# A second Newton step in the reciprocal square root, and QKV weight transfers issued ahead of the LayerNorm loops, in an adaLN transformer layer on eight cores

## What is computed

```python
mod = (_silu(L0_c) @ L0_wmod).reshape(4, 6, 1, -1)      # sa, ca, ga, sb, cb, gb
h = _layernorm(x) * (1 + ca) + sa
q, k, v = h @ Wq.T + bq, h @ Wk.T + bk, h @ Wv.T + bv    # 16 q heads, 8 kv heads of 128
q, k = rope(q), rope(k)
def _softmax_kernel(x, R):
    n = jnp.sqrt(jnp.sum(x * x, axis=-1, keepdims=True))
    x = x / jnp.maximum(n, 1e-06)
    p = jnp.einsum('...d,ed->...e', x, R)
    feats = jnp.concatenate([jnp.sin(p), jnp.cos(p)], axis=-1)
    return feats / math.sqrt(F)
kv = einsum('bhsf,bhsd->bsfd', kp, v);  out = einsum('bhsf,bsfd->bhsd', qp, kv)
x = x + ga * (out @ Wo.T + bo)
h = _layernorm(x) * (1 + cb) + sb
x = x + gb * (sum of top-2 experts of h + shared expert of h)
```

## Time and profile before

| | us |
|---|---|
| median of the 2 timed runs | 3984.06 |
| lowest, highest | 3969.1, 3999.03 |
| profiled execution, its own time | 3891.31 |
| span of its slowest core (core 2) | 3889.8 |
| spans of all eight cores | 3820.8 to 3889.8 |
| TensorE busy, core 2 | 2504.4 (64%) |
| VectorE busy | 1339.4 (34%) |
| ScalarE busy | 379.8 (10%) |
| GpSimd busy | 170.3 (4%) |

### The profile page before, as it was taken

The page is one execution under the profiler, slowest core; times in us unless marked ns, Lnnn a source line. Parts: engine busy times, 40 slices in busy tenths (PEclk is TensorE's granted clock), DMA queues, the critical chain, the costliest instruction groups (busy, mean ns, idle before and its releaser), DMA issues.

```text
span 3889.8 us, 32080 instructions; the slowest of 8 cores (3820.8 to 3889.8 us)
## 1 busy us (share of the span) xinstructions
PE 2504.4 (64%) x10824; PEld 1081.6 (28%) x10824; DVE 1339.4 (34%) x2408; ACT 379.8 (10%) x422; POOL 170.3 (4%) x294
## 2 busy tenths in 40 slices
PE   4349821223972333683399579985899589976886
PEld 1124311111431111231144233432344234432332
DVE  0456255655613454436422022221222122211203
ACT  0121212121111111102100000000000000000000
POOL 0000000000000111000000000000000000000000
PEclk7559955555986566795599789998999899988997
DMA  9513100102334543610143864448543864457547
GB/s 164 103 54 65 25 26 15 28 25 46 65 55 82 103 74 75 165 23 0 41 90 65 169 225 109 87 71 256 159 92 65 200 217 87 92 110 230 159 83 262
DMA packets 84939, 395.09 MB, mean 102 GB/s; under 512 B 7184, under 2 KB 7440, under 8 KB 75312
## 3 DMA queue, kind: packets, MB, share of 16 engines
q0 software_dynamic: 41536, 208.26, 30.8%
q1 hardware_dynamic: 33696, 146.98, 10.8%
q10 hardware_dynamic: 9552, 37.80, 2.8%
HBM read 538.26 MB, written 46.20 MB: 150 GB/s over the span
## 4 chain that ended last, share of the span: by engine, by line
PE 50%; DMA 25%; DVE 13%; issue 8%; ACT 3%; DVEq 0%; POOL 0%; ACTq 0%; POOLq 0%; SPq 0%
PE pb L1034 23%; PE pb L612 9%; PE pb L1110 8%; DMA AW<-wmod 8%; DMA AW<-w2i 5%; DMA AW<-w2scr 4%; PE pb L902 3%; DMA w2scr<-AW 3%; DMA AW<-w1i 2%; DVE AMS L780 2%; PE pb L429 2%; DVE AMS L1122 2%; PE pb L578 1%; PE pb L548 1%; DVE AHT L583 1%
## 5 line engine op out<-in xcount | busy, mean ns | idle before, releaser
L1034 PE MATMUL pb<-AHT,AW 128*128 128x512 bf16 x4608 | 1007.4, 381 | 69.4 <-DMA AW<-w1i 48.5
L1110 PE MATMUL pb<-AW,AOT 128*128 128x512 bf16 x2304 | 586.6, 420 | 287.7 <-DMA AW<-w2i 150.2
L1034 PEld LDWEIGHTS pb<-AHT,AW 128*128 128x128 bf16 x4608 | 450.6, 98 | 626.0 <-issue 94.2
L1110 PEld LDWEIGHTS pb<-AW,AOT 128*128 128x128 bf16 x2304 | 239.9, 106 | 634.5 <-issue 422.2
L612 PE MATMUL pb<-AW,AHT 128*128 128x512 bf16 x1536 | 350.8, 382 | 0.0
L1122 DVE TENSOR_TENSOR AMS<-pb,AMS 128x2048 f32<-128x2048 f32 x40 | 91.7, 2292 | 718.8 <-PE pb L1110 715.0
L578 PE MATMUL pb<-identf,AX 128*128 128x128 f32 x256 | 98.3, 445 | 289.3 <-ACT AX L539 237.2
L429 PE MATMUL pb<-AW,scol 128*1 128x512 bf16 x384 | 135.0, 529 | 143.7 <-DMA AW<-wmod 128.5
L1058 ACT ACTIVATE AMS<-AMS 128x1024 f32<-128x1024 f32 x64 | 67.7, 1057 | 1469.5 <-DVE AMS L1055 1265.0
L1060 DVE TENSOR_TENSOR AMS<-pb,AMS 128x1024 f32<-128x1024 f32 x64 | 78.4, 1225 | 372.2 <-PE pb L1034 372.2
L612 PEld LDWEIGHTS pb<-AW,AHT 128*128 128x128 bf16 x1536 | 143.2, 98 | 182.1 <-issue 25.0
(11 more groups left out here) (148 smaller groups left out, 1649.8 us busy)
## 6 DMA issues: line engine op xcount, KB each, us to landing
AW<-w2scr SPq DMA_DIRECT2D x54, 2048.0 KB, 9.1
AW<-wmod POOLq DMA_DIRECT2D x24, 2048.0 KB, 19.2
w2scr<-AW ACTq DMA_DIRECT2D x18, 2048.0 KB
AW<-w1i POOLq DMA_DIRECT2D x32, 1024.0 KB, 9.3
AW<-w3i POOLq DMA_DIRECT2D x32, 1024.0 KB, 9.3
AW<-w2i POOLq DMA_DIRECT2D x16, 2048.0 KB, 22.5
AX<-xin SPq DMA_DIRECT2D x16, 1024.0 KB, 4.9
AW<-wqt POOLq DMA_DIRECT2D x4, 2048.0 KB, 19.1
```

The lines of the kernel that those rows point to most:

```text
L1034: ins = tt.matmul(pu[:, th * 512:(th + 1) * 512], slot(sl)[:, ic * 128:(ic + 1) * 128], ahtb[:, ic * 1024 + th * 512: ic * 1024 + (th + 1) ...
L1110: ins = tt.matmul(pw[:, ob * 512:(ob + 1) * 512], hebuf[:, hc * 1024 + tau * 128: hc * 1024 + tau * 128 + 128], slot(ws)[:, ob * 512:(ob + ...
```

## The change

Three edits. `emit_rsqrt` makes two Newton steps instead of one. The two GpSimd transfers of a QKV block (weights and bias row) move into a function `emit_qkv_wdma`, and those of blocks 0 and 1 of each half are emitted ahead of the loop that precedes that half's QKV: ahead of the LayerNorm loop for half 0, ahead of the middle of half 0 for half 1. The bias row goes round lanes 4 to 7 like the weights.

```diff
-            for _ in range(1):
+            for _ in range(2):
                 sch.op("vector", lambda v: v.tensor_mul(tmp_f, dst_f, dst_f),
...
-        def emit_qkv_block(sh, ob):
+        def emit_qkv_wdma(ob):
             wname, wbi = wsrc[ob]
             wkey = f"awblk{ob % 2}"
             sch.dma("gpsimd", lambda g, wname=wname, wbi=wbi, ob=ob: g.dma_start(
                 blkbuf(ob % 2)[:].rearrange("p (c n) -> p c n", c=NIC),
                 dram[wname][wbi]), lanes=(4, 5, 6, 7),
                 writes=W(ar_aw, wkey, (ob % 2) * 16384, (ob % 2 + 1) * 16384))
-            isq, isv = ob < 2, ob >= 4
             bsrc = ["bq", "bq", "bk", "bk", "bv", "bv"][ob]
             brow = brows[0:1, (ob % 2) * 512:(ob % 2) * 512 + 512]
-            brkey = f"brow{ob % 2}"
             sch.dma("gpsimd", lambda g, bsrc=bsrc, ob=ob, brow=brow: g.dma_start(
                 brow, dram[bsrc][0:1, (ob % 2) * 512:(ob % 2) * 512 + 512]),
-                writes=[brkey])
+                lanes=(4, 5, 6, 7), writes=[f"brow{ob % 2}"])
+
+        def emit_qkv_block(sh, ob, skip_dma=False):
+            if not skip_dma:
+                emit_qkv_wdma(ob)
...
+        emit_qkv_wdma(0)
+        emit_qkv_wdma(1)
         for t in range(8):
             emit_ln1_tile(0, t, True, None, lnxsA,
...
-            emit_qkv_block(0, ob)
+            emit_qkv_block(0, ob, skip_dma=(ob < 2))
...
+        emit_qkv_wdma(0)
+        emit_qkv_wdma(1)
         for t in range(8):
             if t:
                 emit_mid_B(0, t - 1)
...
-            emit_qkv_block(1, ob)
+            emit_qkv_block(1, ob, skip_dma=(ob < 2))
```

More of the change, by code:

```diff
@@ L595, in emit_qkv_block @@
                 writes=W(ar_aw, wkey, (ob % 2) * 16384, (ob % 2 + 1) * 16384))
-            isq, isv = ob < 2, ob >= 4
             bsrc = ["bq", "bq", "bk", "bk", "bv", "bv"][ob]
             brow = brows[0:1, (ob % 2) * 512:(ob % 2) * 512 + 512]
-            brkey = f"brow{ob % 2}"
             sch.dma("gpsimd", lambda g, bsrc=bsrc, ob=ob, brow=brow: g.dma_start(
                 brow, dram[bsrc][0:1, (ob % 2) * 512:(ob % 2) * 512 + 512]),
-                writes=[brkey])
+                lanes=(4, 5, 6, 7), writes=[f"brow{ob % 2}"])
+        def emit_qkv_block(sh, ob, skip_dma=False):
+            if not skip_dma:
+                emit_qkv_wdma(ob)
+            wkey = f"awblk{ob % 2}"
+            isq, isv = ob < 2, ob >= 4
+            brow = brows[0:1, (ob % 2) * 512:(ob % 2) * 512 + 512]
+            brkey = f"brow{ob % 2}"
             for t in range(8):
```

## The result

The changed kernel takes 3939.48 us (median of 13 runs), the kernel before 3902.73 (12 runs beside it, on the same chip): a ratio of 1.0099 with a 95% interval of 1.0072 to 1.0126. In some executions the cores of one die show a lower granted clock and the time is 70 to 190 us longer; ratios leave these out, and the two timed runs that I took as the level, 3999.03 and 3969.1, are as long as those. So the change costs 37 to 39 us where I forecast 14.4. Two errors of opposite sign stand behind that: the level is 81 us lower than the two runs had it, and the change costs 22 to 24 us more.

The account below looks back on a forecast made before the run. No engine is near full in the middle of half 0: one chain through VectorE, ScalarE and TensorE bounds it. Terms +17.4 + 1.0 - 4.0 + 0 + 0 = +14.4 us on 3984.06 gave 3998.5, range 3940 to 4045.

Parts of the forecast that it names:

- the level: Whole kernel: the median of two timed runs, 3984.06 us, taken as the time before, to which +14.4 was added.
- The second Newton step: Middle of half 0: four added operations cost 1.12 us on 128x16, 1.05 on 128x1; eight tiles give +17.4 us.
- the cover: Middle of half 1: added steps run beside modulation transfers whose waits swallow them; +1 us, bounds 0 and 9.0.
- The transfers of half 0: Before QKV of half 0: second weight block issued near 110, landing near 142.3, shortening VectorE's `xin` wait; 4 us off, bounds 0 and 5.9.
- The transfers of half 1: Middle of half 0: early weights gain nothing, and `v16` behind them still lands in time; cost 0, 8 us or more spare.
- `gac`: Output projection: the `wot` block now waits for the `gac` transfer on its lane; cost 0, with 40 us of cover.
- the 25 us: Middle of half 0: a sign of being wrong was growth under 10 or over 25 us; about 17 was expected.
- the 3 us: Middle of half 1: a sign of being right was its length staying as before within 3 us.
- runs stand otherwise than those two: Whole kernel: timed runs lie more than 50 us from the two used as base, with either sign; chance 0.07.
- Unhidden steps in half 1: Rival, middle of half 1: Newton steps not hidden on cores whose modulation blocks land early; +22.4 us, 4006.5; chance 0.15.
- the clock: Rival, QKV of half 1: the longer middle brings TensorE's full clock back later; 171 us in all, 4169; chance 0.03.
- Weights that pay: Rival, QKV of half 1: early weights save two landings of 16.2 us; -18.0 us, 3966; chance 0.03.

Follow-up runs that it names:

- before_lanes_last: The kernel before with only its order of waits set to the changed kernel's (VectorE, ScalarE, TensorE, then transfer lanes, GpSimd last); ratio 1.0037 to the kernel before.

## Why the prediction was wrong, point by point

**The second Newton step: right, to about a microsecond.** At the same order of waits, with nothing else changed, the middle of half 0 grew by 17.4 (491.7 less 474.3), 17.3 (491.8 less 474.5), 17.3 (499.4 less 482.1) and 17.3 (485.5 less 468.2). That stage starts behind the first tile's reciprocal root, so another 1.1 us lies ahead of it: 18.5 for the 17.4 of the sum. Over all 192 calls on the eight cores the four added operations took a median of 1.12 us on 128x16 and 1.05 on 128x1, as forecast.

**Half 1: the cover held.** In the same comparisons the middle of half 1 grew by 0.6 us and shrank by 2.1, 4.9 and 2.2; I had said 1.0, with bounds of 0 and 9. Two traces of one program differ by 4.3 us in this stage, so all that this shows is that the 9 us of the steps do not come through whole. The steps are taken up where L429 waits less for `wmod`. Its first tile's step, ahead of where I start this stage, goes to the QKV stage, which grew by 0.7 to 1.3 us in those pairs.

**The transfers of half 0: right in size, wrong in one step.** GpSimd and VectorE on core 2 after:

```profile
109.21 0.53 POOL L592 DMA_DIRECT2D AW<-wqt  x1 [10.21 <-PE pb L429]
109.73 0.52 POOL L598 DMA_DIRECT2D brows<-bq  x1
122.65 0.55 POOL L592 DMA_DIRECT2D AW<-wqt  x1 [12.40 <-PE pb L429]
123.20 0.51 POOL L598 DMA_DIRECT2D brows<-bq  x1
```

```profile
145.42 2.28 DVE L511 TENSOR_REDUCE lns<-AX 128x1 f32<-128x2048 f32 x1
```

The bias row no longer waits, but the second block is issued at 122.65, not near 110: it still waits for TensorE, whose matmuls read that half of AW, as `semc_tensor` in the order had said. That is still ahead of the 129.74 at which it was issued before, behind the bias row's wait. It landed 19.0 us later, at 141.7, for 142.3 forecast: one spacing of 13.2 us behind the first block, which landed at 128.5, as the sum had it, so the late issue cost nothing. VectorE's 5.93 us for `xin` are gone. QKV of half 0 starts 3.2 us earlier in the mean over the cores, and 2.7, 4.1, 4.2 and 4.6 in the pairs that differ by the transfers alone, for the 4 that I took.

**The transfers of half 1, and `gac`: right.** Timeline of GpSimd, answering to the earlier trace rows, then the group that answers to the earlier trace rows:

```profile
462.15 0.55 POOL L592 DMA_DIRECT2D AW<-wqt  x1 [29.89 <-PE pb L621]
462.71 0.50 POOL L598 DMA_DIRECT2D brows<-bq  x1
463.31 2.13 POOL L756 DMA_DIRECT2D AMS<-AX  x4
478.42 2.09 POOL L756 DMA_DIRECT2D AMS<-AX  x4 [12.98 <-DMA AMS<-AX]
```

```profile
L859 POOL DMA_DIRECT2D AW<-wot x3 | 2.5, 827 | 93.4 <-PE pb L429 38.2 <-PE pb L915 30.5 <-DMA AHT<-dmod 24.7
```

The first tile's `v16` is issued at 463 and 478 and has landed at 481.9, well ahead of its first reader at 515.05, and the `wot` block waits 24.7 us for `gac` without anyone waiting for it. QKV of half 1 begins at full speed but for its first group, whose row took 5.99 us for 5.11:

```profile
976.10 5.99 PE L618 MATMUL pb<-AW,AHT 128*128 128x512 bf16 x16
982.02 0.39 PE L621 MATMUL pb<-brows,onesr 1*128 1x512 bf16 x1
```

**What the sum missed: two terms.** The step that failed is my reading of the order of instructions. "Nothing else changes on VectorE, and ScalarE's and the sync queue's instructions are the same" holds for the operations, and from it I concluded that nothing else changes. The waits of an instruction are instructions too, and I compared their set and not their sequence, so the sum put the order of waits at nothing. It is 7.6 us in the middle of half 0, and 5.5 in the middle of half 1 (455.9 less 450.4, or up to 9.8 against the other build of the same program, so this one is not sharp). The second is smaller and less sure: in all four pairs that differ by them alone, the moved transfers lose time in the middle of half 1. It is 1.6 and 2.9 us in the two pairs that ran on one chip, 4.3 and 8.0 in those across chips, which gives much of the gain at the start back. Two traces of one program differ by 4.3 us in that stage, so the four suggest the sign and not the size, and the cause is open.

In ratios: 1.0068 for the change with the lanes first, plus 1.0037 less 1.0019 for the order, gives 1.0086, inside 1.0072 to 1.0126; each of the three is known to some 0.002, so this sum agrees but proves little. By stages, the mean core ends 37.9 us later: 1.4 gained up to the middle of half 0, then +25.2 (17.6 Newton, 7.6 order), +2.0 in QKV of half 1, +14.4 in its middle (9.8 from before to `before_lanes_last`, 4.6 from there to the changed kernel), and 2.3 less in the rest. So the middle of half 0 is longer by just over the 25 us, and the middle of half 1 by far more than the 3 us, that I had named as signs.

**The level.** The other step that failed: I added the sum to the median of two runs, 3984.06, and gave 0.07 to "runs stand otherwise than those two". Twelve runs have a median of 3902.73. That chance was too little: the profiled execution, 92.75 us lower, was the better guide, and its own forecast of 3905.7 plus the 20-odd missed microseconds is near the 3933.59 of the profiled execution after.

**The rivals.** Unhidden steps in half 1 (4006.5) and the clock (4169) did not come: granted clocks are 0.51 and 0.99. "Weights that pay" did not either. One sum was off without harm: by its own terms the spare time of `v16` at the usual landing is 19 us and not over 20, and 7.8 where it says 8 or more.

## What to carry to other kernels

When a source edit changes a time and the edited instructions don't account for it, compare the sequence of waits at the instructions that gained idle time, not only the instructions; a scheduler that sorts by an address can give every build another kernel. Pin that order before measuring anything small, or an experiment of 0.3% may measure the order. And put the wait that is signalled last at the end of the list: here one rule for it brought 1%, as much as the change under study cost.

## What the runs showed of the hardware

A TensorE matmul started 146 ns after the end of the VectorE operation it needed, and 106 ns later for each wait that stood behind that one, though those had been satisfied long before: 252, 358 and 464 ns for one, two and three. On TensorE one such wait is a record of 51 ns. A chain of small VectorE operations, each waiting for the one before, stood at 0.28 us from start to start on 128x16, 0.26 on 128x1, each operation being busy for 0.17 to 0.18 and 0.16. The eight cores of one execution agreed to 0.8 us in a stage of 482 us that is bound by such waits (DMA share 0.12), and differed by up to 36 us in one of about 446 us with a DMA share of 0.54.
